# Attention sums: a tile of two heads multiplies its own 34 value columns, and the leftover keys' product comes first

## What is computed

```python
q, k, v = heads(q), heads(k), heads(v)            # 16 heads of 16 features
scores = jnp.einsum('bhtd,bhsd->bhts', q, k)      # 256 tokens, 77 keys; layer 1 adds a relative bias
weights = jax.nn.softmax(scores, axis=-1)
attn = jnp.einsum('bhts,bhsd->bhtd', weights, v)
x = x + jnp.tanh(g) * (attn @ wo)
```

## Time and profile before

| | |
|---|---|
| median of three runs | 2578.39 us |
| the three runs | 2578.39, 2574.0, 2589.82 us |
| span of the profiled execution | 2582.9 us |
| instructions in the profile | 44103 |
| mean granted clock of TensorE | 0.951 |

### The profile page before, as it was taken

One profiled execution on the slowest core, in us unless ns is written; L12 is line 12 of the kernel. 1 busy time (PEld: TensorE's weight loads), 2 busy tenths in 40 slices (PEclk: granted clock), 3 DMA queues, 4 the chain that ended last, 5 costly groups with the idle time before them and its releaser, 6 DMA issues.

```text
span 2582.9 us, 44103 instructions
## 1 busy us (share of the span) xinstructions
PE 2207.2 (85%) x13970; PEld 1819.5 (70%) x14003; DVE 1309.8 (51%) x3668; ACT 751.3 (29%) x1509; POOL 954.7 (37%) x1330
## 2 busy tenths in 40 slices
PE   2899999999999999999999899999809888888884
PEld 1677777777777777777777777777607766677763
DVE  1456555565555556556554655656454433343331
ACT  2122222222222222222222222222234444444432
POOL 1234343343434335343442434434222333333333
PEclk7799998999898999999999999999958999999997
DMA  4000000000000000000010000000053333333332
GB/s 111 2 9 28 27 8 27 16 27 8 27 27 8 27 16 27 8 27 27 9 34 8 27 12 23 27 16 24 15 167 61 60 57 57 57 57 57 59 53 29
DMA packets 93781, 88.28 MB, mean 34 GB/s; under 512 B 26896, under 2 KB 87312, under 8 KB 93752
## 3 DMA queue, kind: packets, MB, share of 16 engines
q0 software_dynamic: 26160, 35.87, 8.1%
q1 hardware_dynamic: 67592, 52.04, 7.4%
HBM read 43.48 MB, written 44.39 MB: 34 GB/s over the span
## 4 chain that ended last, share of the span: by engine, by line
PE 51%; DMA 18%; issue 12%; DVE 7%; POOL 5%; ACT 5%; SPq 1%; POOLq 0%; DVEq 0%; ACTq 0%
PE scores L1086 30%; DMA out<-y,ids 17%; PE bank L1086 16%; POOL sorted_rows L665 3%; PE bank L1154 2%; DVE t_lo L891 1%; DVE biased L968 1%; ACT t_hi L744 1%; ACT routed L779 1%; POOL rstd L612 1%; PE scores L1211 1%; DVE e L965 1%; POOL kb_hi L630 1%; DMA raw<-w_down_t 1%; ACT neg_mx L754 1%
## 5 line engine op out<-in xcount | busy, mean ns | idle before, releaser
L693 POOL DMA_INDIRECT out<-y,ids x136 | 211.6, 1556 | 464.8 <-ACT y L803 281.6
L612 POOL TENSOR_TENSOR rstd<-var,half_power 128x2 f32<-128x2 f32 x128 | 90.0, 703 | 681.0 <-DVE var L878 680.3
L1086 PE MATMUL scores<-vb,pr 128*128 128x136 f32 x2048 | 280.8, 280 | 0.7 <-ACT pr_rest L765 0.7
L891 DVE TENSOR_TENSOR t_lo<-bank,t_hi 128x512 fp32r<-128x512 f32 x192 | 132.1, 688 | 257.6 <-ACT t_hi L744 255.1
L1086 PEld LDWEIGHTS scores<-vb,pr 128*128 128x128 f32 x2048 | 259.2, 191 | 4.5 <-ACT pr_rest L765 0.9
L1086 PE MATMUL scores<-q_hi,kb_hi 128*128 128x256 f32 (+1 forms) x640 | 223.2, 349 | 34.4 <-ACT neg_mx L754 34.4
L1086 PE MATMUL scores<-neg_mx,expand 8*128 8x256 f32 (+1 forms) x640 | 246.5, 385 | 0.0
L744 ACT ACTIVATE t_hi<-bank 128x512 fp32r<-128x512 f32 x192 | 114.6, 597 | 441.7 <-PE bank L1154 441.6
L1070 DVE SCALAR_TENSOR_TENSOR h<-scores,relu 128x512 f32<-128x512 f32 x136 | 94.1, 692 | 274.6 <-ACT relu L797 268.6
L941 DVE TENSOR_REDUCE mx<-scores 128x8 f32<-128x512 f32 x256 | 169.6, 683 | 122.3 <-remote 81.5
L1086 PE MATMUL scores<-up_hi,xt_hi 128*128 x272 | 121.1, 445 | 82.8 <-DVE xt_lo L1064 82.6
(11 more groups left out here) (221 smaller groups left out, 5744.4 us busy)
## 6 DMA issues: line engine op xcount, KB each, us to landing
xe<-sorted_rows SPq DMA_DIRECT2D x136, 128.5 KB, 2.1
x<-x_rows SPq DMA_DIRECT2D x32, 256.0 KB, 2.9
out<-x_end SPq DMA_DIRECT2D x32, 256.0 KB, 3.0
raw<-w_up_t SPq DMA_DIRECT2D x8, 512.0 KB, 4.6
raw<-w_down_t SPq DMA_DIRECT2D x8, 512.0 KB, 4.5
ctx<-ctx_t SPq DMA_DIRECT2D x32, 77.0 KB, 2.7
out<-y,ids POOLq DMA_INDIRECT x136, 3.8
sorted_rows<-routed,place POOLq DMA_INDIRECT x128
```

What stands on the lines that cost most here:

```text
L612: pool.tensor_tensor(rstd[u][:], var[u][:], half_power[:], ALU.pow).then_inc(sem(f"rstd_ready{u}"), 1)
L693: pool.indirect_dma_start(out=acc, out_offset=bass.IndirectOffsetOnAxis(ap=ids[j][:], axis=0), in_=y[j][:], in_offset=None, compute_op=ALU ...
L891: dve.tensor_tensor(t_lo[u][:].rearrange("p k t -> p (k t)"), bankC[:], t_hi[u][:].rearrange("p k t -> p (k t)"), ALU.subtract).then_inc(s ...
L1086: last = pe.matmul(dst, w, m, start=n == 0, stop=n == len(pairs) - 1)
```

## The change

`vb` keeps 34 columns (`PV`) for a tile in place of 136. In `sums`, the leftover keys' product over all 136 columns is issued first and opens the accumulation; each of the four tiles then multiplies its own 34 columns and accumulates onto the slice `j * 34` of the same bank. The number of products stays at five. The set-up data move from `vb` to a tile of their own, `at_setup`, and GpSimd's three waits ahead of the clearing go. The views `values` and the ones write through are adapted to the new stride.

```diff
+PV = 2 * VW
...
-        vb = sb1("vb", [P, 2, 2, G * NJ * GV])
+        vb = sb1("vb", [P, 2, 2, G * NJ * PV])
+        at_setup = sb1("at_setup", [P, 2944])
...
-        expand_raw = vflat[0:HG, 0:KEYS]
-        hot_raw = vflat[0:32, 1280:1280 + LINE]
-        line_sb = vflat[0:H, 2600:2600 + LINE]
-        bias_t_rest_f = vflat[:, 2048:2048 + NC * G * REST].rearrange("p (c g h s) -> p c g h s", c=NC, g=G, h=HG)
+        sflat = at_setup[:]
+        expand_raw = sflat[0:HG, 0:KEYS]
+        hot_raw = sflat[0:32, 1280:1280 + LINE]
+        line_sb = sflat[0:H, 2600:2600 + LINE]
+        bias_t_rest_f = sflat[:, 2048:2048 + NC * G * REST].rearrange("p (c g h s) -> p c g h s", c=NC, g=G, h=HG)
...
-            pool.wait_ge(sem("bias_t_ready"), 2)
-            pool.wait_ge(sem("small_copied"), 5)
-            pool.wait_ge(sem("line_done"), 1)
             pool.memset(vb[:], 0.0).then_inc(sem("vb_zero"), 1)
...
-                        dst = view(vb, (l * 2 + u) * G * NJ * GV + e * VW, [[NJ * GV, G], [GV + 2 * VW, NJ], [1, DH]], e * S0, S0)
+                        dst = view(vb, (l * 2 + u) * G * NJ * PV + e * VW, [[NJ * PV, G], [PV, NJ], [1, DH]], e * S0, S0)
...
-                first = ((l * 2 + u) * G + g) * NJ * GV
-                pairs = [(pr[u][:, g, j, part], vflat[:, first + j * GV:first + (j + 1) * GV]) for j in range(NJ)]
-                pairs.append((pr_rest[u][:, g, part], vr[:, l, u, g].rearrange("p h v -> p (h v)")))
-                last = product(sc[:, c, g * GV:(g + 1) * GV], pairs)
+                first = ((l * 2 + u) * G + g) * NJ * PV
+                pe.matmul(sc[:, c, g * GV:(g + 1) * GV], pr_rest[u][:, g, part], vr[:, l, u, g].rearrange("p h v -> p (h v)"), start=True, stop=False)
+                for j in range(NJ):
+                    last = pe.matmul(sc[:, c, g * GV + j * PV:g * GV + (j + 1) * PV], pr[u][:, g, j, part],
+                                     vflat[:, first + j * PV:first + (j + 1) * PV], start=False, stop=j == NJ - 1)
                 if g == G - 1:
                     last.then_inc(sem(f"pvc_done{u}"), 1)
```

More of the change, by code:

```diff
@@ L589, in _ @@
                     for u in range(2):
-                        pool.memset(view(vb, (l * 2 + u) * G * NJ * GV + e * VW + DH,
-                                         [[NJ * GV, G], [GV + 2 * VW, NJ], [1, 1]], e * S0, S0), 1.0).then_inc(sem("v_ones"), 1)
+                        pool.memset(view(vb, (l * 2 + u) * G * NJ * PV + e * VW + DH,
+                                         [[NJ * PV, G], [PV, NJ], [1, 1]], e * S0, S0), 1.0).then_inc(sem("v_ones"), 1)
                 pool.wait_ge(sem("v_ones"), 4 * (e + 1))
```

## The result

| | before | after |
|---|---|---|
| median | 2584.11 us | 2654.39 us |
| lowest and highest of 4 runs each | 2574.0 to 2595.98 | 2643.47 to 2692.34 |
| span of the profiled execution | 2582.9 us | 2641.5 us |
| mean granted clock of TensorE | 0.951 | 0.903 |

The ratio is 1.0253 with an interval of 1.018 to 1.0326: the kernel became slower by more than a measurement of it can miss. It leaves out the run of 2692.34 us, a slow one, over 1.5% above the fastest of its kernel; the medians contain all runs. The forecast was 2614 us, 1.4% slower, with a range of 2556 to 2665.

The account below looks back on a forecast made before the run. The prediction took TensorE, busy for 2207.2 of 2582.9 us, to bound the kernel. On the profiled span 2582.9 - 6.1 - 1.4 + 43 = 2618.4, less 4.5 for the median, gave 2614 us, range 2556 to 2665.

Parts of the forecast that it names:

- The sign and the cause: Whole kernel: 1.4% slower, because narrow tile products let TensorE's granted clock fall 39 more times; chance of slower 0.57.
- Item 1: Tile products of `sums`: a record falls from 115 to 112 ns, 4 ns saved, 8.2 us over 2048 records (0 to 16).
- columns set the price: Rival for the tile products: weight load hidden, 34 columns cost 29 ns, 132 us kept, 2446 us; chance 0.03.
- Item 2: Wait for `hot_sum` in router halves: takes back the last two products' saving, so 6.1 us are kept (0 to 12.3).
- Items 3 and 4: Leftover keys first in `sums`, and VectorE's value writes in the new layout: each costs or saves 0.
- Item 5: Set-up: GpSimd no longer waits to clear `vb`, so `c_lo` starts 1.4 us earlier (1.0 to 1.5).
- Item 6: TensorE's granted clock in the loop: 39 more falls at 1.1 us each, 43 us lost (0 to 115).
- I take 1.1 for one, nearer to the short one: Price of one clock fall: 1.1 us, chosen between 0.65 for a short low stretch and 2.94 for one twice as long.
- The clock stays: Rival on TensorE's clock: narrow records keep it up as before, only the small savings remain, 2571 us; chance 0.26.
- The falls last long: Rival on the clock: half-clock stretches run on; 2686 us with all 39 at 2.94 us, 2651 with half; chance 0.10.

Follow-up runs that it names:

- router34: Kernel before with leftover keys first and 34-column tile products only in the two router halves of a turn: 2631.83 us, ratio 1.0213 to before.
- others34: Kernel before with leftover keys first and 34-column tile products only in the two halves without the router: 2600.58 us, ratio 1.0095 to before.
- w136: Kernel before with only the order in `sums` changed, leftover keys first, tiles still over 136 columns: 2576.83 us, ratio 0.9986 to before.
- w34: Kernel before with leftover keys first and 34-column tile products, old set-up and `vb` layout kept: 2665.16 us, ratio 1.0344 to before.
- w102: Kernel before with leftover keys first and 102-column tile products, old set-up and `vb` layout kept: 2589.24 us, ratio 1.0048 to before.
- after_fill3: Changed kernel with three unread float32 products of 256 columns added ahead of the wait for `hot_sum`: 2663.79 us, ratio 1.0358 to the kernel before.

## Why the prediction was right, and where it was off

*The sign and the cause: right; the place only nearly.* 39 more falls of the clock were forecast, "the fall at nearly every one of the 30 places" of the wait for `hot_sum` and once a turn in batch row 1, layer 0. The trace has 14 + 14 + 14 in 14 turns, in these three halves, where there were 13 in all. But in the router halves they were to start "around the wait for `hot_sum`", and all start ahead of it, under records without a gap. The forecast took the falls of before, made by that wait, for the model of the new ones; the narrow products need no wait. router34 and others34 show that they belong to the narrow products, w136 and w34 that neither the order nor the set-up and layout do it.

*Item 1, the price of a record: right.* 112 ns from the router's records; measured, 4 ns less per tile record at 102, 68 and 34 columns alike. The router's records with 8 columns and these have the same 112 ns: it is a floor that moving fewer columns does not lower, and the weight load, the same in all of them, is what the forecast put it down to. The Trainium skill, "TensorE: Matmul & The Clock Gate", section "LDWEIGHTS (loading the stationary operand)", gives an estimate of 107 ns for this load; the traces have 112, and the section's rule was the one to follow. That page's "Back-to-back issue gap" gives its formula for the isolated product; the 17 ns estimated by it for 34 columns hold for none of these runs of tile records, and the rival "columns set the price" is out.

*Item 2, what the waits take back: wrong in size.* The wait for `hot_sum` should have grown from 1.6 us by 0.1, and did: 57.5 us in 32 in w102 against 52.6 in w136, 0.15 each; in after the low clock hides it, and in 8 of 32 places TensorE is so late that it does not wait at all. But 6.1 us were to be kept, an undisturbed turn of 109.4 us. It takes 109.72 in w102, 0.04 less than before, so some 0.5 us are kept in the whole loop. The saving was followed through one wait, and the other halves have waits of their own.

*Items 3 and 4: right as far as seen.* w136 has the leftover keys first: 0.9986, not to be told from 1. Slices without narrower products were not run; w102, with slices of 102 columns, needs no longer for an undisturbed turn than before. VectorE's busy time is 1313.5 against 1309.8 us.

*Item 5, the set-up: 0.9 us, not 1.4.* The whole difference of 0.5 lies ahead of `c_lo`: ScalarE's `c_hi` ended at 59.92 instead of the 59.59 taken over from before, and `c_lo` started at 60.10, 0.18 behind it. That `c_hi` is late next, behind the DMA of `ctx`, was named; that it would itself shift was not.

*Item 6, the clock: the mis-sized term.* The step that failed is "I take 1.1 for one, nearer to the short one". The count in the 14 turns rose by 32 (39 were forecast over the loop), but a fall no longer lasts 3.4 us: the 45 last 306.90 / 45 = 6.8 us on average. By halves, one of 3.4 us costs 1.22 us, the longer ones of the router halves 1.52 and 1.88. The falls of before in a router half began 9 us behind the start of `sums`, right where the wide products behind the wait come; those of after begin 3.1 to 6.2 us behind it; the ones within 4.5 us of it last 10.2 us, the others there 6.8. The low stretches sum to 306.90 us where 150 to 250 were forecast. The turns lost 44.7 us, 1.4 for each of the 32 falls more, and the end of part 1 lost 4.9, where +43 less about 6 was forecast.

*The sum.* On the profiled span 2618.4 was forecast, and 2641.5 measured: 23 us short. With the turns of both kernels counted from the first product of a half, 3 of these are the start of the first turn (1.8 late where 1.4 early was forecast), 13 the turns and the end of part 1 (49.7 against 43 - 6.1 = 37 forecast), 5 the last half's `sums` under the low clock, and 2.5 part 2, which the change does not touch and which took 718 to 722 us in the profiles of this study. Of the 13, 5.6 are the saving that was not kept, and the rest is the clock. The measured 2654.39 lies within the range, 11 us below its end. The four runs of after spread over 49 us, more than those of before, and their median lies 13 us above the profiled span. What makes those runs longer stays open. w34 has the larger ratio (1.0344 against 1.0253), but it was taken against faster runs of before; the medians are 0.4% apart, less than the runs of either spread.

*The rivals.* "The clock stays" is out: 306.90 us low against 78.30. "The falls last long" was half right: not 17 us each, but 6.8 on average, as long as the one at 1403.2, for 1.4 us each and not 2.94. Its 2651 us for half of them long are close to what came by luck. The sentence of the Trainium skill, "TensorE: Matmul & The Clock Gate", Part 1, that puts the lower level down to an idle array did not decide here: TensorE was busy for 3.40 of 3.40 us ahead of the falls at 994.5 and 1021.8, and for 1516.99 us of the 14 turns of after where it had been for 1447.91. A stretch full of narrow records lost the clock where one full of wide records kept it; what the chip counts in a record, no run shows.

## What to carry to other kernels

Before narrowing a moving operand, read the distance between starts of the narrowest record over the same stationary block: if it is near the present one, the columns removed were free, and nothing is to be won. Then look at what stands around: in a loop whose clock is only just kept up, fewer columns in the same number of records can take the clock away, and a few short low stretches a turn cost more than the columns would have saved. Follow a saving through every wait of a turn before counting it: here 0.04 us of 0.5 came through. Idle time is not the only thing to look for around a fall: the stretch right ahead of it may be full of records. Filling a wait with work takes falls away only where the clock is still up when the filling starts, and even there it won no time here.

## What the runs showed that was not expected

- The narrow records' wide neighbours pay a part of their saving. In w34 above, the eight tile records take 1235.89 - 1235.08 = 0.81 us, and the leftover pair behind them 1236.20 - 1235.89 = 0.31, where the first leftover pair, behind records of 512 columns, took 0.24. For 34, 68, 102 and 136 columns the eight tile records take 0.81, 0.84, 0.87 and 0.93 us and the pair behind them 0.31, 0.28, 0.25 and 0.23, so that every width below 136 comes to 1.12 us. The starts of single records in w34 show where it goes: the first narrow one behind a wide pair costs only some 35 ns, the next ones 106 to 112 each, and the first wide one behind narrow ones 199 in place of the 119 behind wide ones. The starts fit a weight load that runs beside a wide record and not beside a narrow one; no run here tested that reading.
- The price of a fall is not in proportion to its length and depends on the half. In router halves of after 6.8 us at half clock cost 1.2 to 1.6 us and 10.2 us 1.7 to 2.3; in the second half, with no wait for `hot_sum` behind it, 3.4 us cost some 1.2 and 6.8 us 2.2 to 2.4.
- That difference and after_fill3 fit one reading: the wait for `hot_sum`, which looked like pure loss, shielded the turn against the low clock, and filling it took that away.
